# The last feed-forward layer with its inner values made turned and its norm outside the path

## The reference

```
xn = layernorm(x)                              # no gain, no bias
h  = gelu(xn @ Wfc.T)                          # 1024 inner values, exact gelu
h  = (h - mean(h)) * rsqrt(var(h) + 1e-5) * ln_w + ln_b
x  = x + h @ Wproj.T
```

## Time and profile before

| | us |
|---|---|
| median of 3 runs | 3631.68 |
| the profiled execution's own time | 3622.71 |
| its span | 3620.9 |
| last stage, first work on VectorE | 3461.76 |
| its last addition to `x` starts | 3616.63 |

### The profile page before, as it was taken

The page is one execution under the profiler, slowest core; times in us unless marked ns, Lnnn a source line. Parts: engine busy times, 40 slices in busy tenths (PEclk is TensorE's granted clock), DMA queues, the critical chain, the costliest instruction groups (busy, mean ns, idle before and its releaser), DMA issues. The chain is left out here.

```text
span 3620.9 us, 75209 instructions
## 1 busy us (share of the span) xinstructions
PE 3182.0 (88%) x30384; PEld 2203.4 (61%) x30384; DVE 1830.8 (51%) x4577; ACT 1200.6 (33%) x2371; POOL 917.2 (25%) x754
## 2 busy tenths in 40 slices
PE   8886999999977868878778999789996999899978
PEld 3334555555666854746545555489996886566655
DVE  7886544543233554332586666543334662455543
ACT  1222333333223432311225655322221652244332
POOL 1001533432000000423427878412111110104000
PEclk9998999999989989978889999889998999999989
DMA  4223000001042020634601110278886100111100
GB/s 150 58 67 97 9 9 17 8 8 32 18 55 24 4 52 4 182 99 125 180 18 33 34 30 21 76 269 333 332 323 222 38 8 6 61 49 53 42 9 15
DMA packets 173918, 287.21 MB, mean 79 GB/s; under 512 B 79120, under 2 KB 144197, under 8 KB 164274
## 3 DMA queue, kind: packets, MB, share of 16 engines
q1 hardware_dynamic: 166130, 262.48, 23.5%
q0 software_dynamic: 7488, 20.46, 1.7%
HBM read 244.49 MB, written 28.48 MB: 75 GB/s over the span
## 5 line engine op out<-in xcount | busy, mean ns | idle before, releaser
L2646 PE MATMUL ps<-L_ffn_xsT,arena 128*128 128x128 f32 x2584 | 309.9, 279 | 20.1 <-DVE L_ffn_xsT L2445 14.1
L2646 PEld LDWEIGHTS ps<-L_ffn_xsT,arena 128*128 128x128 f32 x2584 | 301.8, 196 | 23.8 <-DVE L_ffn_xsT L2445 16.8
L161 POOL TENSOR_TENSOR rstd<-nsc,mhalf 112x4 f32<-112x4 f32 (+1 forms) x24 | 40.1, 1669 | 919.6 <-DVE nsc L154 918.7
L820 POOL TENSOR_TENSOR L_xattn_rn<-L_xattn_ss,mhalf 125x16 f32<-125x16 f32 (+1 forms) x64 | 185.8, 2903 | 257.2 <-DVE L_xattn_ss L883 257.2
L3329 POOL TENSOR_TENSOR L_xattn_pT<-L_xattn_pT,L_xattn_keep 125x678 int32<-125x678 int32 x128 | 190.4, 1510 | 71.6 <-ACT L_xattn_pT L3584 71.6
L2544 ACT ACTIVATE L_ffn_silu<-ps,arena 128x128 f32<-128x128 f32 x280 | 102.9, 368 | 268.9 <-PE ps L2646 253.6
L701 PE MATMUL ps<-L_attn_prod,arena 128*32 128x448 f32 (+29 forms) x672 | 157.8, 507 | 27.3 <-DVE L_attn_prod L510 27.0
L2454 DVE SCALAR_TENSOR_TENSOR L_ffn_hT<-ps,arena,L_ffn_silu 128x128 f32<-128x128 f32 x280 | 97.9, 350 | 155.6 <-ACT L_ffn_silu L2544 155.4
L997 PE MATMUL ps<-arena,L_xattn_cT 128*125 128x512 f32 x384 | 166.1, 592 | 0.0
L2323 POOL DMA_INDIRECT L_ffn_rows_out<-L_ffn_ys,L_ffn_dest x78 | 79.7, 1022 | 335.5 <-DVE L_ffn_ys L2463 303.7
L2659 PE MATMUL ps<-arena,L_ffn_hT 128*128 128x256 f32 x646 | 154.1, 383 | 0.1
(11 more groups left out here) (585 smaller groups left out, 6873.1 us busy)
## 6 DMA issues: line engine op xcount, KB each, us to landing
arena<-in_L_ffn_up SPq DMA_DIRECT2D x35, 2056.0 KB
arena<-in_L_ffn_down SPq DMA_DIRECT2D x35, 1152.0 KB
L_xattn_ctxT<-in_ctxT SPq DMA_DIRECT2D x48, 375.0 KB, 3.7
arena<-in_L_ffn_up SPq DMA_DIRECT2D x43, 384.0 KB
L_attn_a<-L_attn_skew SPq DMA_DIRECT2D x16, 784.0 KB, 5.1
L_xattn_ctx<-in_ctx SPq DMA_DIRECT2D x30, 375.0 KB
arena<-L_xattn_kp SPq DMA_DIRECT2D x64, 93.8 KB, 3.3
L_xattn_mask<-in_mask SPq DMA_DIRECT2D x32, 164.1 KB, 8.4
```

Of the source, the lines that this page charges most:

```text
L820: nc.gpsimd.tensor_tensor(rn[0:r, i], ss[0:r, i], core.mhalf[0:r, 0:H], ALU.pow).then_inc(po_r.step("root", i), 1)
L2646: ins = nc.tensor.matmul(ps[:, 2 + b % 4, half * TS:(half + 1) * TS], self.up(i % WU, k, half * HM + m), xsT[:, i % 2, k], start=(k == 0), ...
```

## The change

Only `L3Feed.build` changes.

- The up product is made turned, as in `Mlp`: `widen` writes 128 inner values by 448 tokens, 16 products a chunk; gelu goes into `hT`. No `h`, no transposes of `h`, no copies with gain and bias.
- The norm is written as output = rs * (h @ centred) + bias + x. `centred` is `ln_w * Wproj.T` less a row (1/1024 of `ln_w @ Wproj.T`), made once by 8 instructions on DVE; `bias` is the row `ln_b @ Wproj.T`, spread over the tokens. Both rows come from 16 one-row products on TensorE (8 at output partition 0, 8 at partition 32), two small copies by ScalarE and two products with a row of ones.
- `centred` has a 257th column of ones, so each down product gives the sum of `h` of each token too. The sum of squares: ScalarE squares each `hT[:, i]`, VectorE adds the eight squares into one, and four products of one column each sum it over the partitions (into column 257 of the output's banks). They stand after sequence 0's down products.
- VectorE makes mean and variance from these two columns by five small instructions for each pair of sequences, GpSimd takes the power -0.5, and VectorE adds rs * product to `x`. GpSimd adds `bias` to `x` beforehand.
- ScalarE's and TensorE's chunk 0 stand outside their loops; the turning of chunk c + 1 stands between widen and narrow of chunk c; the down product has banks 4 to 7 for itself. SyncE writes `x` out by two sequences.

```diff
         @block.gpsimd
+            nc.gpsimd.memset(centred[:, :, D:D + 1], 1.0).then_inc(column, 1)
             norm_pool(core, norm)
+            pool.wait_ge(made, 2)
             with pool.Fori(0, NCH) as c:
-                for ln in lns:
-                    ln.pool(pool, ve, po, c)
+                for u in range(U):
+                    x = core.x[0:T, U * c + u, :]
+                    pool.wait_ge(ve_x.sem, ve_x.at(c, "xn", u))
+                    nc.gpsimd.tensor_tensor(x, x, bias[:, :], ALU.add).then_inc(po_b.step("x", u), 1)
+                for p in range(2):
+                    pool.wait_ge(ve_v.sem, ve_v.at(c, f"var{p}"))
+                    nc.gpsimd.tensor_tensor(rs[:, two], var[:, two], core.mhalf[0:T, 0:2], ALU.pow).then_inc(po_r.step("rs", p), 1)
         @block.vector
-            (hidden_norms: statistics, Norm.apply, and turned(): four copies of hT for each sequence)
+            def added(c):
+                for i in range(1, HK):
+                    dve.wait_ge(ac_s.sem, ac_s.at(c, "square", i))
+                    if i > 1:
+                        dve.wait_ge(ve_a.sem, ve_a.at(c, "added", i - 2))
+                    nc.vector.tensor_tensor(sq[:, 0], sq[:, 0], sq[:, i], ALU.add).then_inc(ve_a.step("added", i - 1), 1)
             def outputs(c):
+                for p in range(2):
+                    dve.wait_ge(pe_o.sem, pe_o.at(c, "out", 2 * p + 1))
+                    (mean, raw variance, mean squared, difference, max with EPS: 5 instructions of 112x2)
+                    dve.wait_ge(po_r.sem, po_r.at(c, "rs", p))
+                    for u in range(2 * p, 2 * p + 2):
+                        nc.vector.scalar_tensor_tensor(out=x, in0=ps[0:T, 4 + u, 0:D], scalar=rs[:, u:u + 1], in1=x,
+                                                       op0=ALU.mult, op1=ALU.add).then_inc(ve_o.step("out", u), 1)
+            dve.wait_ge(spread, 1)
+            for i in range(HK):
+                nc.vector.scalar_tensor_tensor(out=centred[:, i, 0:D], in0=self.pr[:, i, :], scalar=self.lw[:, i:i + 1], in1=ps[:, 6, 0:D],
+                                               op0=ALU.mult, op1=ALU.subtract).then_inc(made, 1)
             with dve.Fori(0, NCH - 1) as c:
-                hidden_norms(c)
                 normalise(c + 1, False)
+                added(c)
                 outputs(c)
         @block.scalar
+            def bend(c, first):
+                for i in range(HK):
+                    act.wait_ge(pe_u.sem, pe_u.at(c, "up", i))
+                    nc.scalar.activation(hT[:, i], ps[:, i % 4, 0:N4], ACT.Gelu).then_inc(ac_g.step("gelu", i), 1)
+                    act.wait_ge(ac_g.sem, ac_g.at(c, "gelu", i))
+                    nc.scalar.activation(sq[:, i], hT[:, i], ACT.Square).then_inc(ac_s.step("square", i), 1)
+            nc.scalar.activation(line[0:1, :], ps[0:1, 4, 0:D], ACT.Copy, scale=1.0 / H).then_inc(lines, 1)
+            nc.scalar.copy(line[32:33, :], ps[32:33, 4, 0:D]).then_inc(lines, 1)
+            keep_turned(0)
+            bend(0, True)
+            with act.Fori(1, NCH) as c:
+                keep_turned(c)
+                bend(c, False)
         @block.tensor
+            def widen(c):   (as Mlp.widen: 8 x 2 products of 448 columns)
+            def narrow(c, first):
+                for u in range(U):
+                    for i in range(HK):
+                        if u == 0:
+                            ten.wait_ge(ac_g.sem, ac_g.at(c, "gelu", i))
+                        ins = nc.tensor.matmul(ps[0:T, 4 + u, 0:D + 1], hT[:, i, u * T:(u + 1) * T], centred[:, i, :], start=(i == 0), stop=(i == HK - 1))
+                    if u == 0:
+                        ten.wait_ge(ve_a.sem, ve_a.at(c, "added", HK - 2))
+                        for w in range(U):
+                            ins = nc.tensor.matmul(ps[0:T, 4 + w, D + 1:D + 2], sq[:, 0, w * T:(w + 1) * T], core.ones[:, 0:1], start=True, stop=True)
+            for i in range(HK):
+                nc.tensor.matmul(ps[0:1, 4, 0:D], self.lw[:, i:i + 1], self.pr[:, i, :], start=(i == 0), stop=(i == HK - 1))
+                ins = nc.tensor.matmul(ps[32:33, 4, 0:D], self.lb[:, i:i + 1], self.pr[:, i, :], start=(i == 0), stop=(i == HK - 1))
+            turn(0, True)
+            ten.wait_ge(lines, 1)
+            nc.tensor.matmul(ps[:, 6, 0:D], core.ones[0:1, :], line[0:1, :], start=True, stop=True).then_inc(spread, 1)
+            ten.wait_ge(lines, 2)
+            nc.tensor.matmul(ps[0:T, 7, 0:D], core.ones[32:33, 0:T], line[32:33, :], start=True, stop=True).then_inc(spread, 1)
+            widen(0)
+            turn(1, False)
+            narrow(0, True)
+            with ten.Fori(1, NCH - 1) as c:
+                widen(c)
+                turn(c + 1, False)
+                narrow(c, False)
+            widen(NCH - 1)
+            narrow(NCH - 1, False)
```

More of the change, by code:

```diff
@@ L4863, in build @@
         sb = run.sbuf
[L4864 to L4874, removed]
+        xn, xT, hT, sq = sb("xn", [T, U, D]), sb("xT", [128, KD, N4]), sb("hT", [128, HK, N4]), sb("sq", [128, HK, N4])
+        centred, line, bias = sb("centred", [128, HK, D + 1]), sb("line", [64, D]), sb("bias", [T, D])
+        mean, square, var, rs = (sb(t, [T, U]) for t in ("mean", "square", "var", "rs"))
+        norm, written, made, column = (core.semaphore(t) for t in ("norm", "written", "made", "column"))
+        sums, lines, spread = core.semaphore("sums"), core.semaphore("lines"), core.semaphore("spread")
+        pe_t, pe_u = Progress(core, "tensor_xT", ("xT", KD)), Progress(core, "tensor_up", ("up", HK))
+        pe_s, pe_o = Progress(core, "tensor_squares", ("squares", 1)), Progress(core, "tensor_out", "out")
+        ac_t, ac_g, ac_s = Progress(core, "scalar_xT", ("xT", KD)), Progress(core, "scalar_gelu", ("gelu", HK)), Progress(core, "scalar_square", ("square", HK))
+        ve_x, ve_a, ve_o = Progress(core, "vector_xn", "xn"), Progress(core, "vector_added", ("added", HK - 1)), Progress(core, "vector_out", "out")
+        ve_v = Progress(core, "vector_var", *(x for p in range(2) for x in ((f"mean{p}", 1), (f"raw{p}", 1), (f"square{p}", 1), (f"diff{p}", 1), (f"var{p}", 1))))
+        po_r, po_b = Progress(core, "pool_rs", ("rs", 2)), Progress(core, "pool_bias", "x")
         block = run.block
@@ L4959, in _, with turn @@
             ten.wait_ge(run.arrived, run.loads)
-            def feed(c, first):
+            def turn(c, first):
+                for k in range(KD):
+                    if not first:
+                        ten.wait_ge(ac_g.sem, ac_g.at(c - 1, "gelu", 4 + k))
+                        core.stand(ten)
+                    for u in range(U):
+                        if k == 0:
+                            ten.wait_ge(ve_x.sem, ve_x.at(c, "xn", u))
+                        ins = nc.tensor.transpose(ps[:, k, u * T:(u + 1) * T], xn[:, u, k * 128:(k + 1) * 128], core.ident[0:T, 0:T])
+                    ins.then_inc(pe_t.step("xT", k), 1)
@@ new lines, in widen @@
+            def widen(c):
+                for i in range(HK):
+                    if i >= 4:
+                        ten.wait_ge(ac_g.sem, ac_g.at(c, "gelu", i - 4))
+                    for k in range(KD):
+                        if i == 0:
+                            ten.wait_ge(ac_t.sem, ac_t.at(c, "xT", 1 if k else 0))
+                        ins = nc.tensor.matmul(ps[:, i % 4, 0:N4], self.fc[:, k, i * 128:(i + 1) * 128], xT[:, k],
+                                               start=(k == 0), stop=(k == KD - 1))
+                    ins.then_inc(pe_u.step("up", i), 1)
@@ new lines, in narrow @@
+                    ins.then_inc(pe_o.step("out", u), 1)
+                    if u == 0:
+                        if not first:
+                            ten.wait_ge(ve_o.sem, ve_o.at(c - 1, "out", U - 1))
+                        ten.wait_ge(ve_a.sem, ve_a.at(c, "added", HK - 2))
+                        core.stand(ten)
+                        for w in range(U):
+                            ins = nc.tensor.matmul(ps[0:T, 4 + w, D + 1:D + 2], sq[:, 0, w * T:(w + 1) * T], core.ones[:, 0:1], start=True, stop=True)
+                        ins.then_inc(pe_s.step("squares"), 1)
```

116 lines of the change are left out of this document (37 added, 79 removed).

## The result

The changed kernel takes 3593.55 us (median of 4 runs, 3591.05 to 3600.61). The kernel before took 3629.64 in the 4 runs beside them. The ratio is 0.9895 with a 95% interval of 0.9882 to 0.9907: faster, by 36 us or 1.05%.

What follows compares the result with a forecast made beforehand. TensorE was taken as the bound. First up product to last down product 152.4 becomes 115.6 (-36.8), tail +2.2, last transfer -0.4: -35.0 us from the median 3631.7 gives 3597, range 3587 to 3610.

Steps and rivals of the forecast that it cites:

- The bound: The changed stage: TensorE bounds it, losing about 8 us a chunk to needless turning or waiting; new chunk 27.7 against 37.99.
- The prologue: Stage start, TensorE: one-row sums (work 3.7), turning 0.77, two spread products 2 x 0.6; widen starts 5.6 us later than before.
- Rival B: Prologue dearer: one-row products don't overlap (+3.2), or don't raise the clock (work at half speed); 3602 us, chance 0.20.
- The covers: Narrow: transposes and sequence 0's down products (4.2 us, last chunk 3.5) hide the squares' chain; slack 1.5 or more.
- The squares' wait: TensorE's wait for VectorE's last addition of squares, 1.9 to 2.0 us after the last up product; forecast to cost nothing.
- rival C: Widen: ScalarE or VectorE sets the pace, gelu, wait and Square taking 1.75 instead of 1.24; 3604 us, chance 0.12.
- The tail: Stage end: last product to last output 2.7 us, 2.2 more than before; last transfer 0.4 less.
- Rival D: Widen: a table load of 1.283 us at every change between gelu and Square; +73, 3670 us, chance 0.04.
- break-even: ScalarE's table loads: from about 1.1 us more for each of 32 pieces (35 / 32) the change becomes slower.
- The forecast of the median: Whole kernel: 35.0 us subtracted from the median 3631.7, not the profiled execution, giving 3597; chance 0.62.

Runs made afterwards that it cites:

- e5: Kernel before with the inner norm left out whole, output not the reference's: stage 139.1 us against 159.1, ratio 0.994 to the kernel before.
- e1: Changed kernel with both sums of one-row products in the same column group (output partition 0): stage 125.7 us against 121.8.
- e4: Changed kernel with one more Square of the same input for each piece, into a spare tile: stage 121.7 us against 121.8.
- e2: Changed kernel with the squares' four one-column products ahead of sequence 0's down products instead of behind them: stage 133.5 us against 121.8.
- e10: e2 with 16 transposes of the identity filling TensorE's wait in front of the squares' products: stage 129.9 us against 133.5.
- e3: Changed kernel with the exponential in place of Square, so ScalarE alternates two tables: stage 199.7 us against 121.8.
- e6: Changed kernel with the two rows added by VectorE, summed by two TensorE products, replacing the one-row products: stage 120.4 us, ratio 0.9897 to the kernel before.
- e8: e6 with the up product in bfloat16 (tokens as high and low part), squares after all gelus: stage 102.5 us, ratio 0.984 to the kernel before.
- e9: Changed kernel, one-row products kept on TensorE, with e8's bfloat16 up product: stage 100.0 us, ratio 0.9815 to the kernel before.

## Why the prediction was right

| term | forecast | measured |
|---|---|---|
| first normalisation to widen(0) | 7.8 | 6.6 |
| widen(0) to the last down product | 110.0 | 109.5 |
| last product to last output | 2.7 | 2.7 |
| last output to the end of the span | 3.5 | 3.0 |
| stage | 124.0 | 121.8 |

*The bound.* TensorE was the bound in both, and its stream became gapless, as `L3_mlp` had shown in the earlier trace rows. This carried the forecast: widen 12.03 against 12.13, turning 0.76 against 0.77, down products 14.0 against 13.9, squares 0.71 against 0.9. The 5.80 us in front of the last transposes, the transposes and the exchange of banks all went; e5 puts 20.0 us on the norm's chain and 17.3 on the order. The prediction took the 2.75 of the last transposes as their work; about 1.1 of it was the clock of 0.50 after the wait. The sum didn't suffer, since it started from the measured stage before.

*The prologue* was sized 1.2 too dear for this execution. The sums overlap fully and took 5.0 us instead of 5.75: the clock rose 3 us after TensorE began and not 4 (some 0.6 of the difference), and the work was 3.5 instead of 3.7. Turning and the spread products, which overlap each other, took 1.6 instead of 2.0. Rival B's first half (no overlap) is refuted by the trace and priced by e1 at 3.9. Its second half, the clock, lives in small: the same prologue took 6.6 us in the changed kernel and 6.5 in e4, but 8.0 in e2 and e10 and 7.9 in e3. So the forecast of 7.8 is as near to what this code takes as the 6.6; that the profiled execution had the early clock is luck, worth 1.4 us.

*The covers.* The squares' wait was never reached: in the chunk shown the last of VectorE's additions ended at 3515.57 and TensorE came to its squares at 3517.73, 2.2 us later. Taken away, the cover is worth 1.31 to 1.95 a chunk and, beyond my account, a possible fall of the clock. ScalarE had more in hand than I said (0.45 rather than 0.28 a piece, e4), so rival C was further off than its chance.

*The tail* came out right in sum, 2.69 against terms of 2.73, but in part because errors cancel: the five small instructions took 0.76 instead of 0.9, the handover from GpSimd 0.13 instead of 0.05. The end of the span came 0.9 sooner after the last output instead of 0.4: the last 224 KB landed in 2.3 us, where the forecast used the 2.9 of 256 KB in the earlier trace rows.

*Rival D* did not happen and had the right price: e3 shows 1.28 for each change of table, 78 us in all against 73; part of the surplus is down products at a lower clock (their mean in the trace's groups is 461 ns against 380), and 1.3 is its prologue. Its break-even was too low, though: 35 / 32 = 1.1 us a piece forgets that the first 0.28 are hidden. One load a piece would have made ScalarE 1.05 + 1.28 = 2.33 against 1.50, 27 us over 32 pieces, and the change would still have gained some 8 to 10 us, an estimate from e3 and e4. And the prediction passed over the nearest row: the stage itself had eight loads of 1.28 before, in each chunk one with its copy (L4945) and one ahead of its first gelu (L4949), beside TensorE's products; the changed stage has one in all.

*The forecast of the median.* 3597 against 3593.55, a gain of 35.0 against 36.1 by the medians and 37.4 by the stage. The 31.7 between the two profiled executions themselves would have misled: 5.5 us of drift lie in stages that did not change.

## What to carry to other kernels

Look in the same trace for a stage that already runs the new order, and take its start-to-start times, not mean durations: the steady chunk then comes out to 1%. What is left to err on is the prologue, where each engine is cold and where work taken from one engine comes back as half clock or as lateness of another (e6, e8). Where a factor per row and a mean can be moved behind a product, the chain of statistics leaves the bounding engine's path for the price of one column and a few small products, and here of a prologue and 2.1 us at the end.

## What the runs showed of the hardware

- A stretch of 1.31 us without work on TensorE was followed in two chunks by a granted clock of 0.85 and 0.58 in the next two stretches of 3 us, which cost 1.7, more than the stretch itself; stretches of 1.43 and 1.95 in the other two were not. With 16 transposes in it the down products took 13.98 us in all four (e2, e10). In the kernel before, waits of 4.2 to 4.3 us left a clock of 0.50 for the work behind them in all four chunks.
- The same 16 one-row products at the stage's start took 4.9 to 5.0 us in two traces and 6.3 to 6.5 in four, as the clock rose from 0.50 after 2.8 to 2.9 us or after 5.5 to 6.0 (changed kernel, e4; e2, e3, e9, e10).
- Two fp32 products with one-column weights in different column groups run in the time of one (0.43 us for the two at full clock, and 0.43 for each where they stand in one group), although each is two instructions (changed kernel, e1).
- Activations of 128x448 that don't need each other's result follow after 0.48 us, though each shows 0.58; one that needs the result before it starts just after its end. A gelu and two Squares of it fit in 1.50 (e4).
- A table load costs 1.28 us and the next activation starts 0.01 to 0.02 after it (e3).
- While GpSimd adds to `x` (2.9 us for four), VectorE's four normalisations of 112x256 take 2.21 us, against the 1.38 that four take at the stage's start with GpSimd nearly idle; it had the time. In e5, where GpSimd adds nothing, none of the 16 takes over 0.41, where the longest here takes 0.82.
